# A two-layer relational graph attention on one core: other seams, another operand order in the last stage, and a rebuilt weight preparation

## The reference, cut to what matters

```python
def rgat_conv(x, W, q, k, b, src, dst, etype, heads, out_ch, n_nodes):
    xr = jnp.einsum('nd,rdf->rnf', x, W)               # 3 relations
    oi = xr[etype, dst]; oj = xr[etype, src]
    alpha = jax.nn.leaky_relu(oi @ q + oj @ k, 0.2)
    m = segment_max(alpha, dst); e = exp(alpha - m[dst])
    a = e / (segment_sum(e, dst)[dst] + 1e-16)
    msg = (a[:, :, None] * oj.reshape(-1, heads, out_ch)).reshape(-1, heads * out_ch)
    return segment_sum(msg, dst) + b
h = elu(rgat_conv(x, W1, q1, k1, b1, ..., heads=4, out_ch=192))
o = rgat_conv(h, W2, q2, k2, b2, ..., heads=1, out_ch=768)
return layernorm(x + o)                                # 1250 nodes used, 40000 edges, 768 features
```

## Time and profile before

| | us |
|---|---|
| median of 3 runs | 1352.9 (1347.56 to 1354.49) |
| the profiled execution's own time | 1352.16 |
| its span, first to last instruction | 1350.4 |
| PE busy | 1295.7 (96%) |
| DVE busy | 1069.7 (79%) |
| ACT busy | 769.7 (57%) |

### The profile page before, as it was taken

One profiled execution on the slowest core, in us unless ns is written; L12 is line 12 of the kernel. 1 busy time (PEld: TensorE's weight loads), 2 busy tenths in 40 slices (PEclk: granted clock), 3 DMA queues, 4 the chain that ended last, 5 costly groups with the idle time before them and its releaser, 6 DMA issues.

```text
span 1350.4 us, 19310 instructions
## 1 busy us (share of the span) xinstructions
PE 1295.7 (96%) x7042; PEld 1168.5 (87%) x7042; DVE 1069.7 (79%) x1447; ACT 769.7 (57%) x1291; POOL 6.5 (0%) x21
## 2 busy tenths in 40 slices
PE   7989999999989999999999999999979999999995
PEld 6876665666669999999999999999969999999994
DVE  1579989999939989989989976868736667867874
ACT  3345542322159979979979964238534445555552
POOL 1000000000000000000000000000000000000000
PEclk9689999999999999999999999999999999999997
DMA  9212013111153333333333226964477866677561
GB/s 324 72 71 89 24 43 123 47 49 49 37 203 98 104 98 98 99 97 98 100 94 95 63 66 199 294 217 155 165 228 258 271 219 203 218 238 237 190 208 38
DMA packets 84984, 188.38 MB, mean 140 GB/s; under 512 B 8221, under 2 KB 59230, under 8 KB 84898
## 3 DMA queue, kind: packets, MB, share of 16 engines
q1 hardware_dynamic: 84608, 186.49, 41.8%
q0 software_dynamic: 192, 0.57, 0.1%
q10 hardware_dynamic: 98, 0.16, 0.0%
HBM read 147.59 MB, written 39.61 MB: 139 GB/s over the span
## 4 chain that ended last, share of the span: by engine, by line
PE 79%; DVE 13%; ACT 4%; DMA 2%; issue 2%; SPq 0%; ACTq 0%; DVEq 0%
PE ps L1129 23%; PE ps L1074 23%; PE ps L910 14%; PE ps L933 9%; PE ps L984 4%; DVE arena L1254 2%; PE ps L892 2%; DVE arena L1310 2%; PE ps L880 2%; DMA arena<-in_L_gnn_W 1%; DVE arena L1314 1%; ACT arena L686 1%; ACT arena L687 1%; DVE ps L1382 1%; DVE misc L1264 1%
## 5 line engine op out<-in xcount | busy, mean ns | idle before, releaser
L1074 PE MATMUL ps<-arena 128*128 128x193 f32 x2400 | 398.1, 328 | 1.8 <-DVE arena L1314 1.5
L1074 PEld LDWEIGHTS ps<-arena 128*128 128x128 f32 x2400 | 393.6, 190 | 4.2 <-DVE arena L1314 3.6
L910 PE MATMUL ps<-arena,xT 128*128 128x384 f32 (+1 forms) x720 | 246.2, 490 | 0.2 <-issue 0.2
L686 ACT ACTIVATE arena<-arena,misc 128x640 f32<-128x640 f32 x240 | 197.2, 822 | 30.9 <-DVE arena L1310 23.1
L910 PEld LDWEIGHTS ps<-arena,xT 128*128 128x128 f32 x720 | 131.6, 190 | 78.6 <-issue 2.3
L1310 DVE TENSOR_TENSOR arena<-arena 128x1280 f32<-128x1280 f32 x120 | 178.3, 1486 | 24.8 <-ACT arena L687 23.8
L687 ACT ACTIVATE arena<-arena,misc 128x640 f32<-128x640 f32 x240 | 196.1, 817 | 0.0
L1314 DVE SCALAR_TENSOR_TENSOR arena<-arena,Ct 128x1280 f32<-128x1280 f32 x120 | 179.2, 1493 | 14.0 <-DVE arena L1310 9.4
L1129 PE MATMUL ps<-g_hi,x2a 128*128 128x416 f32 (+1 forms) x540 | 155.4, 357 | 10.2 <-DVE g_lo L1469 8.8
L1254 DVE SCALAR_TENSOR_TENSOR arena<-arena,misc 128x1250 f32<-128x1250 bf16 x108 | 155.7, 1510 | 2.2 <-ACT arena L638 2.2
L1129 PE MATMUL ps<-g_hi,x2b 128*128 128x416 f32 (+1 forms) x540 | 152.2, 351 | 0.0
(11 more groups left out here) (172 smaller groups left out, 1479.4 us busy)
## 6 DMA issues: line engine op xcount, KB each, us to landing
x2a<-xr_d SPq DMA_DIRECT2D x41, 768.0 KB, 4.4
x2b<-xr_d SPq DMA_DIRECT2D x41, 768.0 KB, 4.4
arena<-xr_d SPq DMA_DIRECT2D x120, 193.0 KB, 2.4
xr_d<-stg SPq DMA_DIRECT2D x60, 384.0 KB, 3.2
arena<-ab_d SPq DMA_DIRECT2D x12, 1280.0 KB, 6.3
xr_d<-bb SPq DMA_DIRECT2D x60, 193.0 KB, 2.4
arena<-in_L_gnn_W SPq DMA_DIRECT2D x5, 2304.0 KB, 9.6
arena<-in_L_gnn_W SPq DMA_DIRECT2D x7, 1152.0 KB, 6.9
```

The lines of the kernel that those rows point to most:

```text
L686: nc.scalar.activation(e1[t % 5][:, h, :], abr[:, r, h, :], ACT.Exp, bias=qk1t[:, t, col + R * H:col + R * H + 1])
L910: last = mm(unit1_bank(u)[:, 0:w], xT[:, kt, t * P:(t + 1) * P], v, start=kt == 0, stop=kt == KT - 1)
L1074: last = mm(bank1(g, i)[:, o:o + HD + 1], e1[t % 5][:, h, i * P:(i + 1) * P], xring[t % NX][:, o:o + HD + 1], start=False, stop=True, skip ...
```

## The change

It has these parts.

- **Weight products with the operands exchanged.** The 8 columns of q1 and k1 become the stationary operand and the transposed weights the moving one, 128 columns; the product has 8 rows, so each relation is copied out twice (`wqs`) and transposed back by 6 small transposes (`wq_transposes`, L920). Eight blocks instead of ten stand before the pairs, the others in pairs 0 to 22, two in five pairs.
- **x transposes through three banks** (`XBK`), the first of them behind the copy of weight block 5.
- **First two steps of layer 1's attention beside the last units.** Step 0's exponentials stand before the copy of unit 58, step 1's before that of unit 59 (in buffers of their own, `e1_first`).
- **Row maxima of layer 2 in two units.** Four banks for the transposes (`MKB2`), five tiles a unit instead of three; the shifts' transposes stand in the middle of unit 54 instead of before unit 57, and SP stores and reloads the shifts at unit 54.
- **Attention of layer 2 with the operands exchanged.** The weights are stationary (128 destinations), the features moving (384 columns, and 2 columns of ones beside them that give the sum of the weights). Ten destination tiles in parts of 4, 3 and 3, two PSUM banks each; no copies and transposes back, no running sum. A stored feature row is 776 instead of 768 wide; the ones are written once by two DMAs. All 90 feature tiles are loaded, no slot is kept.
- **First two steps' weights of layer 2's attention** are made beside units 57 and 58, and PE waits per tile for the banks that the last units used.
- **Rows out tile by tile**: a tile's rows start when its own last matmul is done (`o_done`).

```diff
-    CUTS = [(112, 112, 112, 80), (112, 112, 112, 80), (112, 112, 98, 96)]
+    XO = 8
+    XW = 2 * (F + XO)
+    CUTS = [(128, 128, 128, 128), (128, 128, 128), (128, 128, 98)]
-        MK2_AT, MK2_N, AB2_AT = 52, 3, 57
+        MK2_AT, MK2_N, AB2_AT = 52, 5, 54
+        MKB2 = (7, 0, 1, 2)
+        ROWS_AT, STAT_AT, BIAS_AT = 1, 3, 24
+        TILE_BANKS = ((0, 1), (2, 7), (4, 5), (6, 3))
+        TILE_PAIR = [(0, 1, 2, 3), (0, 1, 2), (3, 0, 1)]
-        PRE = 10
-        WT_AT = {3 * (i - PRE): i for i in range(PRE, R * KT)}
+        PRE = 8
+        WT_AT = {5 * (i - PRE) // 2: i for i in range(PRE, R * KT)}
...
+            for a in range(2):
+                sp.dma_start(xr2_d[:, :, a, F:F + XO].rearrange("n p c -> p n c"), onesf[:, :].unsqueeze(1).broadcast_to([P, RS, XO])).then_inc(S["wide_out"], 16)
...
             def wq_out(i):
-                act.wait_ge(S["wq_done"], i + 1)
-                nc.scalar.activation(o, ps[6 + i % 2][:, 0:2 * H]..., copy).then_inc(S["wq_ready"], 1)
+                if kt == KT - 1:
+                    act.wait_ge(S["wq_done"], i + 1)
+                    for b in range(2):
+                        last = nc.scalar.activation(wqs[0:2 * H, b * HF:(b + 1) * HF], ps[6 + b][0:2 * H, 0:HF], copy)
...
-                if kind == 0 and i == U1 - 1:
-                    act.wait_ge(ab_in[0], 16)
-                    exp_step(0, 0, 0)
+                if kind == 0 and i >= U1 - 2:
+                    if i == U1 - 2:
+                        act.wait_ge(ab_in[0], 16)
+                    exp_step(0, 0, i - U1 + 2)
...
+                if u == NU - 3:
+                    exponentials(0)
+                if u == NU - 2:
+                    exponentials(1)
+                    upper(0)
...
             def wq_product(i):
-                    last = mm(ps[6 + i % 2][:, 0:2 * H], WT[i % 2][:, ft * P:(ft + 1) * P], qv1[:, ft, :],
+                    last = mm(ps[6 + kt // 3][0:2 * H, kt % 3 * P:(kt % 3 + 1) * P], qv1[:, ft, :], WT[i % 2][:, ft * P:(ft + 1) * P],
...
                 for kt in range(KT):
+                    if u == AB2_AT and kt == KT // 2:
+                        ab_transposes(L2)
...
-                    for k in range(KT):
-                        for m, (x_, a) in enumerate(((xs[:, k * P:(k + 1) * P], hi), (xs[:, k * P:(k + 1) * P], lo), (xs[:, F + k * P:F + (k + 1) * P], hi))):
-                            last = mm(ps[k][:, 0:w], x_, a, start=j == 0 and m == 0, stop=j == RS - 1 and m == 2)
+                    for i, (d0, d1) in enumerate(SUBS[g]):
+                        if n == 0:
+                            pe.wait_ge(S["t_evac"], U1 + max([u + 1 for u in range(NU - NB2, NU) if BANK2[u % NB2] in TILE_BANKS[i]] + [0]))
+                        if g and j == 0:
+                            pe.wait_ge(S["o_sum"], M0[q] + TILE_PAIR[q].index(p) + 1)
+                        for m, (a, x0) in enumerate(((hi, 0), (hi, F + XO), (lo, 0))):
+                            for b in range(2):
+                                wide = HF + 2 if b and x0 == 0 else HF
+                                last = mm(banks[b][0:k, 0:wide], a, xs[:, x0 + b * HF:x0 + b * HF + wide], start=j == 0 and m == 0, stop=j == RS - 1 and m == 2)
...
-                z = zacc[g % 2][:, 0:w]
-                    V.tensor_tensor(z, z, v, ALU.add).then_inc(S["z_acc"], 1)
...
             for g in range(NPART):
                 for j in range(RS):
-                    attention2(g, j)
+                    if g or j >= 2:
+                        attention2(g, j)
                     if g:
+                        if j == ROWS_AT:
+                            for i in range(NS[g - 1]):
+                                rows2(g - 1, i)
...
             lower(NPART * RS - 1)
-            dve.wait_ge(S["a_used"], RING + NST + NPART * RS)
-            for k in range(KT // 2, KT):
-                V.tensor_copy(oT[:, k, 0:d1 - d0], ps[k][:, 0:d1 - d0]).then_inc(S["ot_dve"], 1)
```

More of the change, by code:

```diff
@@ L170, in rgat @@
         x_sb = Ct[:, :, :].rearrange("p a b -> p (a b)")[:, 0:2 * NT * F].bitcast(F32).rearrange("p (t f) -> p t f", t=NT)
+        wqs = take(F)
         B0_AT = ARENA - KT * (HF + QC)
@@ L193, in rgat @@
         assert e1_at + 4 * 2 * DH >= 2 * WS and e1_at <= WS
-        hst = take(DT * HF).rearrange("p (t f) -> p t f", t=DT)
-        hmn = take(DT * HF).rearrange("p (t f) -> p t f", t=DT)
+        hst_, hmn_ = take(DT * HF), take(DT * HF)
+        hst, hmn = (v.rearrange("p (t f) -> p t f", t=DT) for v in (hst_, hmn_))
+        e1_first = [v[:, 0:2 * DH].rearrange("p (h d) -> p h d", h=2) for v in (hst_, hmn_)]
         abr_at = pos[0]
@@ L543, in _ @@
                 if g == 0 and 8 <= j < 8 + 2 * NXR and j % 2 == 0:
-                    load_x((j - 8) // 2 // NSUB, (j - 8) // 2 % NSUB)
-                if g and j == STORE_AT + NSUB:
-                    for m in range(NXR + (g - 1) * NSUB, min(NXR + g * NSUB, NPART * NSUB)):
-                        load_x(m // NSUB, m % NSUB)
+                    m = (j - 8) // 2
+                    load_x(0 if m < NS[0] else 1, m - (0 if m < NS[0] else NS[0]))
+                if g == LAST and j == 8:
+                    for i in range(NS[LAST]):
+                        load_x(LAST, i)
                 if j >= NT and j % NT == 0 and g < LAST:
@@ L553, in _ @@
                     load_ab2(g, R - 1)
-                if g and STORE_AT <= j < STORE_AT + NSUB:
+                if g and STORE_AT <= j < STORE_AT + NS[g - 1]:
                     store_out(sp, g - 1, j - STORE_AT)
-            for i in range(NSUB):
+            for i in range(NS[LAST]):
                 store_out(sp, LAST, i)
-            sp.wait_ge(S["o_out"], 16 * NSUB * NPART)
+            sp.wait_ge(S["o_out"], 16 * M0[NPART])
         @block.gpsimd
@@ L664, in _ @@
                     wq_out(WQ_AT[pair - 1])
+                if pair - 1 == max(WQ_AT) + 1:
+                    wq_columns(R - 1)
                 for n in steps0(pair - 1):
@@ L784, in _, with exponentials, upper @@
                 w2_upper(1, i)
+            def exponentials(n):
+                g, j = divmod(n, RS)
+                r, t = divmod(j, NT)
+                w = PARTS[g][1] - PARTS[g][0]
+                if t == 0:
+                    act.wait_ge(ab_in[r], 16 * (NG1 + g + 1))
+                if n >= NG:
+                    act.wait_ge(S["a_ready"], NST + n - NG + 1)
+                nc.scalar.activation(g1[n % NG][:, 0:w], ab2r[:, r, 0, 0:w], ACT.Exp, bias=qk2t[:, t, R + r:R + r + 1])
+                nc.scalar.activation(g2[n % 2][:, 0:w], ab2r[:, r, 1, 0:w], ACT.Exp, bias=ks2[:, t, r:r + 1]).then_inc(S["e_ready"], 1)
+            def upper(n):
+                d0, d1 = PARTS[n // RS]
+                act.wait_ge(S["am_ready"], n + 1)
+                if n >= NG:
+                    act.wait_ge(S["a_used"], RING + NST + n - NG + 1)
+                nc.scalar.activation(g_hi[n % NG][:, 0:d1 - d0], g1[n % NG][:, 0:d1 - d0], copy).then_inc(S["ah_ready"], 1)
             masks = 0
@@ L989, in _ @@
                     wq_product(WQ_AT[pair])
+                if pair == max(WQ_AT) + 1:
+                    wq_transposes(R - 1)
                 for n in steps0(pair):
@@ L1092, in _ @@
                         mk2_transpose(t)
[L1093 to L1094 removed]
                 unit(u)
             pe.wait_ge(S["ab_rows"], 2)
[L1097 to L1116 removed]
+            for g in range(NPART):
                 for j in range(RS):
                     n = g * RS + j
[L1119 to L1120 removed]
                     pe.wait_ge(S["a_ready"], NST + n + 1)
```

296 lines of the change are left out of this document (130 added, 166 removed).

## The result

| | before | after |
|---|---|---|
| median, us | 1350.84 (1347.56 to 1354.49, 4 runs) | 1333.28 (1330.95 to 1333.69, 4 runs) |
| the profiled execution: time, span, mean clock | 1352.16, 1350.4, 0.975 | 1330.95, 1329.1, 0.989 |

The ratio is 0.9868, 95% interval 0.9845 to 0.9891. That is faster by more than the 0.5% that a measurement here can tell; 17.6 us by the medians and 21.3 by the two spans, where 31 were forecast. The changed kernel measured again, beside other kernels, had 1332.59 and 0.9861 (0.9836 to 0.9886).

A forecast was written before the change was run, and what follows sets the result against it. It took PE as the bound: full in the long stages, with time to gain from its work, its waits at seams and its clock. Seven terms sum to -30.7 us, 1352.2 to 1321.5; 8-in-10 range 1308 to 1342.

The forecast's parts named there:

- term A: Weight preparation and first pairs: earlier flag and a loop at the high clock; -15 us, bounds -25 to +17.
- C: Two DMAs writing ones in 32-byte pieces ahead of the ring's reloads in layer 1's attention; +2 us, upper bound +40.
- E: Seam into layer 2's attention: PE waits 3.1 us instead of 8.85, as the shifts' trip ends inside the units; -5.8 us.
- the likeliest forecast: Whole kernel: all terms as summed, 1321.5 us, with its own range 1314 to 1330; chance 0.54.
- rival 1: First pairs: the clock stays as it was; 1334 at the old mix, 1353.5 at the low level throughout; chance 0.22.
- B: Seam into layer 1's attention: earlier exponentials let PE start at once, step 2 4.3 us earlier; -4.3 us.
- Rival 4: Before step 5 of layer 1's attention: writes of ones hold up the ring, +40 instead of +2, 1359.5 us; chance 0.05.
- D: Row maxima of layer 2, units 52 to the last: transposes and waits take 4.8 us instead of 7.9; -3.1 us.
- F: Body of layer 2's attention: 1800 matmuls at about 0.176 us, two new waits at parts' ends, some low clock; +3.9 us.
- rival 3: Body of layer 2's attention goes by the count of matmuls or waits for feature loads; +20, 1342 us; chance 0.07.
- G: Rows out at the kernel's end: it ends 12.9 us behind the last matmul instead of 21.3; -8.4 us.
- Rival 2: Everything overlaps: weight preparation and first pairs at DVE's pace, no wait at layer 2's attention seam; 1309 us; chance 0.12.

The follow-up runs named there:

- experiment 2: The changed kernel with the weight products of the kernel before (8 columns stream, transposed weights stationary), each block's product copied out at once; 1335.44 us, ratio 0.9872.
- experiment 5: The changed kernel with weight products one pair later and the last small transposes of the products and their copy one pair later still; 1325.21 us, ratio 0.9804.
- experiments 9: The changed kernel itself, unedited, measured again beside other kernels in five runs; 1332.59 us, ratio 0.9861 to the kernel before.
- experiment 10: The changed kernel with the edits of experiment 5, later second and third pairs of layer 2 feature loads, and a part's rows one step later; 1317.56 us, ratio 0.9756.
- experiment 11: The changed kernel with layer 1's attention exponentials in the old order (step 0 before unit 59's copy, step 1 behind it); 1335.98 us, one run.
- Experiment 12: The changed kernel with layer 2's row maxima again at three tiles a unit and the shifts' transposes in unit 57 instead of 54; 1338.67 us, one run.

## Why the prediction was right, and where its sizes were off

The direction, the range and most places were right; the gain is 21.3 of the 30.7 us forecast on the same footing. The missing 9.4 us are those of term A. That the other errors cancel (C 2 better, E 2 worse) is luck. And the time alone would have misled: 1333.3 lies outside the likeliest forecast's own 1314 to 1330 and next to the 1334 of rival 1, whose mechanism did not come about.

Term A's stretch in the changed kernel, from the first pair to the first transform, and the pairs' matmuls in it (six a pair):

```profile
47.65:101.75 54.10, 45.72 (x385) 35.20 (x385) 36.46 (x56) 25.44 (x81) 0.20 (x4) 0.97 0.28 99
L1014 PE MATMUL ps<-arena 128*128 128x240 bf16 x162 | 20.4, 267 | 4.0 <-DVE arena L1227 4.0
```

- **A, -15 forecast, -5.6 measured: the mis-sized term.** The flag's matmul came at 45.14 (45.2 forecast). The clock did what was chosen: 1.00 from 52 us on, and experiment 2 shows that the exchange of the operands does it; the mechanism of rival 1 is out. What failed is "with 2 for unevenness between two-deep buffers". From the first pair to the first transform PE waits 8.4 us of 54.1, where 2 were put: 4.4 for ScalarE's copy of the transposed weights, 1.7 for one-hots, 1.4 for the copy of the products, 0.9 at the first transform. Its work is 45.7 where the sum has 38.4 and 3.5 for the low clock, 41.9: the stretch has 27 pairs (162 matmuls) and not 26, a pair there takes 0.72 to 0.79 and not 0.61, a product 1.41 to 1.48 and not 1.29; only the low clock is cheaper, 1.6 and not 3.5. The sum had PE's work and DVE's pace but no chain through ScalarE: two pairs between a block's transposes and its product are cover at 1.21 us a pair and too few at 0.61. The trace of before could have told: from 67 to 107 us, where its clock was high in part, PE waits 3.4 us in seven places for the same copy (L614), and from 50 to 67, at the low clock, never. The edit of experiment 5 brings back 5.0 of it (7.6 between experiments 9 and 10, where the clock fell in one and not in the other). The wait on the one-hots was not tried.
- **B, -4.3: -4.0**, by the mechanism given (experiment 11).
- **C, +2: 0.** The price is half of the upper estimate from reads, 11.6 ns and not 25, and PE waits for no reload. Rival 4 is out; at four times the pieces PE does wait. (Its sum has a slip: 51.2 less 8.6 of cover is 42.6 and not 40, and against the other terms' 32.7 the turning point is 86 ns and not 91.)
- **D, -3.1: -2.75.** The size is right; the working had spread it over banks and fewer interruptions. Experiment 12 shows that the fewer interruptions gave nothing; 2.0 us are waits on reductions that the banks took away.
- **E, -5.8: -3.8.** The mechanism was the one named (SP's loads ahead of the stores, staging slots); the copy of unit 58 was expected to wait, and that of unit 57 waited too, 5.35 us. Not priced was the low clock behind such a wait, 2.4 us, which showed up in F.
- **F, +3.9: +3.3**, with parts that stood in for each other: the two waits were 1.8 us and not 3.5, the low clock cost 2.4 and not 1.5. 0.176 a matmul, 1800 of them by columns and not by count: rival 3 is out.
- **G, -8.4: -8.8.** The last matmul to the end is 12.5 us (12.9 forecast).

The prediction's words on transposes and the clock need a correction. The 24 transposes at 27.0 have the durations of the low level, but the profile of the kernel before prints 1.00 there, as it does from 8 us on, although products take 2.36. So up to its first change the printed clock of that profile can't be used, and the level has to be read from durations. And the trace does not agree with the rule cited for that row, that transposes do not raise the clock. There the next transposes are at the fast pace, 0.136 each (first line below). In the changed kernel PE comes out of a wait of 6.72 us at 0.50 and does nothing but transposes from 32.48 to 40.3, and the clock rises among them:

```profile
32.20 1.09 PE L965 MATMUL ps<-ident,Ct 128*128 128x128 f32 x8
32.48:36.00 3.52, 3.52 (x19) 3.52 (x20) 2.17 (x5) 1.20 (x2) 0.00 (x0) 0.50 0.58 210
38.50:39.00 0.50, 0.43 (x4) 0.19 (x2) 0.47 (x2) 0.50 (x2) 0.00 (x0) 1.00 0.00 0
```

The measurement decides: fp32 transposes do raise the clock here. The sum did not rest on the rule.

Rival 2, "everything overlaps", did not come about: it has A at VectorE's pace, -25, where the changed kernel has -5.6 and experiment 10 -12.0 (180.37 less 168.40). That experiment 10 comes near its 1309 with 1317.6 is in part the work of places that it does not name (the rows at a part's end, the low clock behind the seam).

## What to carry to other kernels

When an engine is to become twice as fast in a stretch, recount every hand-over there in its new time: work placed "two pairs later" covered a copy at the old pace and not at the new one. Price a wait of PE at a seam as the wait plus the slow matmuls behind it (5.07 and 2.4 us here). Before a load is issued early, look at which stores share its queue and engines and who needs the slots that these free.

## What was not expected of the hardware

- A busy PE at the low clock: from 52 to 62 us 10.00 of 10.00 us busy at 0.50 with products of 8 columns (experiment 2); with products of 128 columns 1.00 from 52 to 92 us, though PE is busy for 34.80 of these 40 us only.
- The same instructions at either clock: of ten profiles with the same short waits near 100 us, six fell to the low level there and four did not; from the first transform on it cost 1.7 to 2.6 us.
- fp32 transposes alone brought the clock back: from 32.48 us PE does nothing else, and the clock is 0.50 up to 38 and 1.00 from 38.5 on. The profiles of all twelve experiments show such a rise between 35 and 38.5 us.
- Writes of 32 bytes to DRAM at 11.6 ns each or less per DMA engine with all 16 full.
